# A two-layer graph network on one core: the products of ones ahead of TensorE's waits are taken out of both passes

## What is computed

```python
seg_sum = segment_sum(edge_attr, row, N); seg_max = segment_max(edge_attr, row, N)
seg_mean = seg_sum / maximum(cnt, 1.0);   seg_max = where(cnt > 0, seg_max, 0.0)
h = concatenate([seg_sum, seg_max, seg_mean, u[batch]], axis=1)
x = x + relu(h @ W1 + b1) @ W2 + b2
h = maximum(layernorm(x), 0.0)
x = x + relu(segment_sum(h[src], dst, N) @ W.T + b)
```

## Time and profile before

| | |
|---|---|
| runs | 1616.1, 1617.33, 1629.52 us; median 1617.33 |
| the profiled execution: span from first to last instruction | 1620.5 us |
| TensorE busy / weight loads | 1140.7 us (70%) / 858.5 us (53%) |
| DVE / ACT / POOL busy | 1007.6 (62%) / 393.6 (24%) / 758.5 us (47%) |
| mean granted TensorE clock | 0.802 |
| matmuls of ones (L1422), into `p_t` and `p_u` | 133.8 and 127.8 us busy |

### The profile page before, as it was taken

How to read it: one execution, slowest core, us unless ns; L and a number is a source line. 1 busy time by engine, 2 the same in 40 slices (tenths; PEclk the granted TensorE clock), 3 DMA queues, 4 the chain that set the end, 5 groups by cost and what they waited for, 6 DMA issues and landing times.

```text
span 1620.5 us, 23845 instructions
## 1 busy us (share of the span) xinstructions
PE 1140.7 (70%) x5924; PEld 858.5 (53%) x5924; DVE 1007.6 (62%) x2540; ACT 393.6 (24%) x1174; POOL 758.5 (47%) x823
## 2 busy tenths in 40 slices
PE   0121278868888878888878912787778777878889
PEld 0110146655666656666656611666666656656667
DVE  9888775655666656665656523555556565655565
ACT  0710433333333333333323201111111111111110
POOL 2000455544554555454544066555546555565540
PEclk9975568879888888888878955787878788787779
DMA  1000135766666666576656652677767777767867
GB/s 39 0 0 1 46 74 126 166 141 157 162 166 155 171 162 160 143 172 165 164 145 160 156 148 62 140 157 162 164 133 172 156 154 156 159 149 156 182 145 159
DMA packets 490722, 218.16 MB, mean 135 GB/s; under 512 B 421915, under 2 KB 453631, under 8 KB 490581
## 3 DMA queue, kind: packets, MB, share of 16 engines
q1 hardware_dynamic: 357352, 134.87, 35.9%
q10 hardware_dynamic: 108141, 62.41, 14.2%
q0 software_dynamic: 25088, 19.32, 8.1%
HBM read 136.97 MB, written 79.45 MB: 134 GB/s over the span
## 4 chain that ended last, share of the span: by engine, by line
PE 30%; DVE 20%; another core or an unknown queue 14%; issue 11%; ACTq 8%; DMA 7%; ACT 7%; SPq 2%; POOL 0%; DVEq 0%; POOLq 0%
PE p_t L1417 5%; DMA records<-rec 5%; PE p_m L1405 4%; ACTq L709 4%; PE p_t L1422 3%; PE p_u L1417 3%; ACT hid L720 3%; DVE shared L1152 3%; PE p_u L1422 3%; DVE hn L1221 2%; PE p_z L1397 2%; DMA win<-records 2%; ACTq L701 2%; PE p_z L1417 2%
## 5 line engine op out<-in xcount | busy, mean ns | idle before, releaser
L568 POOL DMA_INDIRECT xa<-in_edge_attr_dram,gi x392 | 373.6, 953 | 452.3 <-DVE feats L1135 131.9
L587 POOL DMA_INDIRECT xa<-node_table,gi x392 | 370.9, 946 | 309.3 <-issue 171.0
L1152 DVE TENSOR_TENSOR shared<-p_m,rel 112x1024 f32<-112x1024 f32 x98 | 120.0, 1225 | 205.7 <-remote 164.5
L1133 DVE TENSOR_TENSOR_SCAN feats<-c_rows,feats,p_g 64x512 f32<-64x512 f32 x97 | 122.9, 1267 | 131.3 <-DMA c_rows<-rows_src 75.7
L720 ACT ACTIVATE hid<-p_z,bias_z 128x512 f32<-128x512 f32 x98 | 112.0, 1143 | 238.5 <-issue 206.9
L1448 PE MATMUL p_g<-ident,hn 128*128 128x128 f32 x196 | 53.3, 362 | 132.2 <-issue 82.8
L1397 PE MATMUL p_z<-feats,w_s 96*128 96x512 f32 x196 | 133.5, 770 | 6.7 <-DVE feats L1135 6.7
L1422 PE MATMUL p_t<-one 128*128 128x256 f32 (+1 forms) x228 | 133.8, 673 | 4.6 <-issue 4.6
L1422 PE MATMUL p_u<-one 128*128 128x512 f32 x230 | 127.8, 642 | 3.8 <-issue 3.8
L1405 PE MATMUL p_m<-w_s,hid 128*128 128x64 f32 x784 | 127.1, 314 | 0.0
L1152 DVE TENSOR_TENSOR oneh<-p_m,rel 112x1024 f32<-112x1024 f32 x98 | 120.1, 1225 | 10.1
(11 more groups left out here) (272 smaller groups left out, 1788.5 us busy)
## 6 DMA issues: line engine op xcount, KB each, us to landing
win<-records SPq DMA_DIRECT2D x980, 28.9 KB
records<-rec ACTq DMA_DIRECT2D x196, 132.0 KB
node_table<-dout SPq DMA_DIRECT2D x49, 512.0 KB
din<-in_x_dram SPq DMA_DIRECT2D x48, 512.0 KB
din<-node_table SPq DMA_DIRECT2D x43, 512.0 KB
out_dram<-dout SPq DMA_DIRECT2D x43, 512.0 KB
c_rows<-rows_src ACTq DMA_DIRECT2D x47, 384.0 KB
win<-records ACTq DMA_DIRECT2D x588, 28.9 KB
```

The lines of the kernel that those rows point to most:

```text
L568: g.indirect_dma_start(out=xa[n % XRING][:, t, 0:FE], out_offset=None, in_=edge_attr, in_offset=bass.IndirectOffsetOnAxis(ap=gi[0][:, BT * ...
L587: g.indirect_dma_start(out=xa[k % XRING][:, t, :], out_offset=None, in_=T, in_offset=bass.IndirectOffsetOnAxis(ap=gi[1][:, BT * n + t:BT * ...
L1133: v.tensor_tensor_scan(f[0:64, :], c[0:64, at:at + BLK], p_g[n % 2][0:64, :], first[0:64], ALU.mult, ALU.add)
L1152: v.tensor_tensor(hots[side][m % HRING][0:WP, :, :], nodes[0:WP, 0:UNIT].unsqueeze(1).to_broadcast([WP, PER, UNIT]), near.unsqueeze(2).to_ ...
```

## The change

The helper `stream` and its two calls are removed: in `expand`, which both passes use, and in the loop of pass 2 with the wait that stood ahead of it. Nothing else differs.

```diff
                 if side == 1 or m >= 2:
                     pe.wait_ge(added, max(k - len(ring) + 1, BLOCKS * side))
-                stream(to, BLK)
                 pe.wait_ge(hot_ok, k + 1)
                 for s in range(PER):
                     last = mm(to[:, D * s:D * (s + 1)], hots[side][m % HRING][:, s, :], win[k % WRING][:, s, 0:D], start=True, stop=True)
                 last.then_inc(expanded, 1)
-
-            def stream(bank, width):
-
-                mm(bank[:, 0:width], one[:, :], one[:, :].unsqueeze(1).to_broadcast([P, width // P, P]), start=True, stop=True)
...
                     if valid(n - DST_EXP):
                         expand(1, n - DST_EXP)
-                    if valid(n - DST_EXP) and valid(n - DST_EXP + 1):
-                        pe.wait_ge(added, max(BLOCKS + n - DST_EXP + 1 - len(p_e[1]) + 1, BLOCKS))
-                        stream(p_e[1][(n - DST_EXP + 1) % len(p_e[1])], BLK // 2)
                     if valid(n - DST_CONV):
                         conv(n - DST_CONV)
```

## The result

| | before | after |
|---|---|---|
| median (runs), us | 1618.12 (12) | 1638.8 (12) |
| lowest and highest, us | 1608.65, 1629.52 | 1629.71, 1656.93 |
| ratio after / before, 95% interval | | 1.0098 (1.0067 to 1.0129) |
| span of the profiled execution, us | 1620.5 | 1645.9 |
| mean granted TensorE clock | 0.802 | 0.606 |

The change makes the kernel slower by about 1%. The forecast was 1748 us with a range from 1640: the direction was right, the size was not, and the time lies just under the range. Ratios are made from runs within 1.5% of the fastest run of the same kernel; on the chip of the first four experiments the kernel before ran once in 1596.63 us with a median of 1623.67, so there the ratios lie some 0.8% above the quotients of the medians, and both are given.

The account below looks back on a forecast made before the run. The prediction took TensorE to bound pass 1 and a cycle with eight gathers, not TensorE's clock, to pace pass 2. From 1620.5, +124 (pass 1), 0 (pass 2) and +8 (tail) gave 1752, less 3 stated as 1748 us; range 1640 to 1815.

Parts of the forecast that it names:

- it does not come back: Without ones, TensorE's clock falls at its first long wait of pass 1 and stays low, near 0.50, in both passes.
- The forecast's own sign of being wrong: Pass 1: a mean clock above 0.6 would show that the ones were not what lifts it.
- The price of the low level: Pass 1 at the low clock without ones: TensorE's work sums to 8.15, say 8.2 us per block, before waits.
- the forecast's lower end: Likeliest case with no waits in pass 1: block 8.2 us, pass 1 +78 us, 1703 us in all.
- 78 to 155 us: Pass 1: TensorE time saved directly by removing ones if the clock stayed as it is, 0.86 to 1.70 us per block.
- waits: Pass 1: TensorE's waits before layer 2, 1.07 us per block before, taken as 0.5 after, with ends 0 and 1.07.
- Pass 2: Pass 2 with gathers: TensorE at the low clock needs 9.3 us for two blocks, inside the 12.86 us cycle: change 0.
- The tail's +8: Tail after the gathers of pass 2: 49 us grows to 57 us at the low clock, +8 us.
- Rival 1: Pass 2 gets quicker because TensorE's signals reach DVE sooner: at most 123 us, half taken, 1690 us; chance 0.08.
- rival 3: Pass 2 loses its pairing, one block per cycle, 7.85 us against 6.43: +122 us, 1870 us; chance 0.08.
- Rival 2: Pass 1: the clock comes back and the ones' time is saved: -113 us at most, half taken, about 1560 us; chance 0.06.
- Rival 4: No change: gathers pace pass 1 too, which needs a clock that half recovers: about 1620 us; chance 0.04.

Follow-up runs that it names:

- the first four experiments: Ones out in pass 1 only (1.0191), in pass 2 only (1.0095); next block's turn moved behind pass 1's expansion, without ones (1.0562) and with them (1.0098).
- e3: The kernel after, with the next block's turn in pass 1 moved from ahead of the expansion to behind it: 1700.69 us, ratio 1.0562.
- e5: The kernel before, with three instead of four gathers per block in pass 2: 1519.1 us in one execution.
- e6: The kernel after, with three instead of four gathers per block in pass 2: 1538.85 us in one execution.

## Why the forecast was right in direction and wrong in size

**The step that failed: "it does not come back".** The forecast took it that without ones the clock falls at the first long wait and stays down in both passes. In pass 2 it did, 0.50 to the end. In pass 1 it came back 22 times. The forecast rested on the earlier trace rows, two busy stretches at 0.50 that hold layer 2, layer 1 and the turn, and on the earlier trace rows, an expansion of pass 2, where neither layer 1 nor a turn stands just ahead. What the clock rose behind in after, layer 1 and turn with an expansion right behind them, could not be seen in the trace of before: there a product of ones always stood between turn and expansion. The rises that were put down to ones were read from the only arrangement that the trace had. One sign was there. The second stretch of the earlier trace rows ends at 597.30, inside the turn; just past it, in before:

```profile
596.53 1.06 PE L1390 MATMUL p_g<-ident,xa 128*64 128x128 f32 x4
597.38 1.14 PE L1422 MATMUL p_t<-one 128*128 128x512 f32 x2
```

```profile
597.00:597.60 0.60, 0.60 (x4) 0.56 (x3) 0.00 (x0) 0.05 (x1) 0.60 (x1) 0.50 0.55 113
597.60:598.00 0.40, 0.40 (x2) 0.16 (x2) 0.37 (x1) 0.40 (x1) 0.14 (x1) 0.98 0.79 141
```

The clock rose at 597.62, when ones had run for 0.24 us and the turn had ended 0.03 us before. A stretch that stops where the ones start, or ahead of it, could not show such a rise, so the earlier trace rows was no proof that layer 1 and the turn do not lift the clock.

The forecast's own sign of being wrong, a mean clock above 0.6 in pass 1, is what happened (0.67).

The Trainium skill's page "TensorE: Matmul & The Clock Gate", section "Part 1: The HAM clock gate (the "warmup" mystery)", says that activity releases the throttle. After's pass 1 bears this out in part, 5.40 us busy of 5.40 at 0.50 and then 0.99; e3, busy 745.32 of 747.00 us at 0.50, does not, and the measurement decides: a busy TensorE alone was not enough here.

**The price of the low level was right.** The forecast summed 8.2 us per block for a TensorE without ones at 0.50; e3, where that state holds, has 8.19 in one block and 8.25 on average, and took 1700.69 us where the forecast's lower end was 1703. (The forecast's own sum, 1620.5 + 124 + 8 less 3, is 1749.5; the 1748 it states is about 1 us off, which changes nothing.) After is a mixture. Its records give TensorE 89 us of pauses in pass 1, 57.5 of them at the higher level: 0.63 us per block there and 0.35 at the lower one. At 34% of 7.55 us, 2.58 us per block pass at the higher level; less 0.63 that is 1.95 / 4.33 = 45% of the blocks, and the rest, (4.97 - 0.35) / 8.2 = 56%. For before the same working, with pauses of 0.80 and 0.40, gives (5.17 - 0.80) / 5.19 = 84% and (2.18 - 0.40) / 9.9 = 18% (9.9 is 8.2 and the ones' 1.70). Both add up to about one, so the prices of the two levels and the pauses account for both kernels. The ones cost TensorE 0.86 to 1.70 us in each block and had 84% of the blocks run at the higher level instead of 45%. The two nearly cancel: over pass 1 the ones cost 78 to 155 us, as the forecast had it, and give that back with 18 us on top in this pair of executions (8 to 22 by the table above).

**The term that was mis-sized: waits.** 0.5 us per block was taken for the low state. In e3 they are 1.7 / 91 = 0.02: a TensorE at the low level is later than `hid` in every block but a few. Where the clock comes back, they do too; in after, 246 to 931:

```profile
L1403 PE MATMUL p_m<-nc,one_b 3*128 3x256 bf16 x91 | 30.6, 336 | 83.8 <-ACT hid L720 61.4 <-issue 22.2
```

83.8 / 91 = 0.92 per block, against the 1.07 of the earlier trace rows. That the wait came out under 1 us, as the forecast's list has it, is thus no support for its reason. With waits at their lower end, 0, the forecast's sum is 1703, for the state that e3 shows.

**Pass 2: right, and for the reason given.** Its gathers' stretch moved by 0.4 us at a clock of 0.50, within the scatter of the table above. Two blocks still take 12.9 us on average, and there are still cycles of 12.86 us with eight gathers in them; DVE's one-hots and POOL's first and last gather of one cycle in after, to be read beside the earlier trace rows:

```profile
1327.74 1.22 DVE L1152 TENSOR_TENSOR shared<-p_m,rel 112x1024 f32<-112x1024 f32 x1 [3.34 <-PE p_t L1416]
...
1340.60 1.22 DVE L1152 TENSOR_TENSOR shared<-p_m,rel 112x1024 f32<-112x1024 f32 x1 [4.65 <-remote]
```

```profile
1329.23 0.94 POOL L587 DMA_INDIRECT xa<-node_table,gi  x1 [1.99 <-DVE shared L1152]
...
1338.05 0.95 POOL L587 DMA_INDIRECT xa<-node_table,gi  x1 [0.30 <-issue]
```

e5 and e6 show the pacing. But this cycle is no longer the usual one: groups of just eight gathers, each start at most 1.5 us behind the one before, stand 33 times in before and 18 times in after, where waits break up the others. DVE's waits have moved as well. Before, they were

```profile
L1152 DVE TENSOR_TENSOR shared<-p_m,rel 112x1024 f32<-112x1024 f32 x98 | 120.0, 1225 | 205.7 <-remote 164.5 <-PE p_u L1417 20.3 <-PE p_t L1417 9.7
...
L1141 DVE TENSOR_TENSOR rel<-win,base_f 112x8 f32<-112x8 f32 x196 | 29.8, 152 | 103.3 <-DMA win<-records 77.2 <-issue 25.6
```

and in after 81.7 us at the one-hot of pass 2 and 178.3 at `rel` (both passes together), mostly for the windows. The forecast did not see that; the length of the stretch held all the same. The tail's +8 was +6.1.

**The rivals.** Rival 1 (pass 2 quicker) and rival 3 (its pairing lost) did not happen. Rival 2 had the mechanism that did, a clock that comes back; half of it came (34% of pass 1 at the higher level, where the rival asked for more than half), not enough to be faster, since before stays at the higher level twice as long. Rival 4, a clock that half recovers, had the outcome, 1620 against 1638.8 measured, with a chance of 0.04; but its other half, that gathers pace pass 1, is not what holds it: in e3 pass 1 follows TensorE. The range was too narrow below because a clock that recovers in part was given almost no weight, though no row of before showed the order of work that the change makes.

**What stays open.** Why the clock rises behind one layer 1 and turn and not behind the next (22 of the 59 blocks that came to it at the lower level), and why the same three pieces in another order never lifted it in 91 blocks, these runs do not settle; they show the effect of the order, not its cause. Nor do they show which of the pieces lifts it.

## What to carry to other kernels

Products that only keep TensorE's clock up are worth their time only so far as the real work would not lift it by itself, and this must be judged from the order that the work will have without them, which the trace of before may not contain. Where the clock hangs on what stands next to what, moving one small step can cost more than the products: here some 58 us for a turn of 0.86 us at another place. In a stage that another engine paces, as POOL's gathers pace pass 2 here, the clock may halve at no cost that can be measured, and only its tail shows it.

## What the runs showed of the hardware

- TensorE stayed at the low level for 747 us while busy for 745.32 of them (e3), and rose to the high level within a few blocks' time again and again with the same instructions in another order (after).
- Every one of the 22 rises of pass 1 in after lies inside an expansion, between 0.09 us before and 0.86 us behind the end of the turn that follows layer 1. They came in 22 of the 59 blocks that began their turn at the lower level; with ones behind the turn, in 28 of 28 (before).
- In the cycles of pass 2 shown, DVE's start that ends a cycle comes about 1.6 us after POOL's last gather ends (1338.05 + 0.95 = 1339.00 to 1340.60 in after; 1.66 in before). What DVE waits for in that time, no run tested.
